# When the scatters of the message stage may begin: TensorE's signals a whole epoch ahead in place of half an epoch

## The chip, the core and the metric
The kernel runs on one core of one Trainium2 chip. The metric is the device time of one launch in microseconds (us). The engines are TensorE (PE), VectorE (DVE), ScalarE (ACT), GpSimd (POOL) and SyncE (SP); each runs its own program in order, and they meet only through semaphores.

## The reference
The kernel computes two message-passing layers of a graph network in float32 on 6250 nodes and 200000 edges, which are sorted by their destination.

The first layer takes the features of each edge's `dst` node and 32 attributes of the edge, and forms a tensor product of 160 values; the messages are added up by the edge's `src` node:

```
tp       = fctp_messages(node_features[col], edge_attr_tensor, W1, W2, W3, W4)
messages = tp @ Wm + bm
agg      = segment_sum(messages, row, N_NODES)
upd      = concatenate([node_features, agg]) @ Wu + bu
x        = layernorm(x + node_features + upd)
```

The second layer gathers by `src`, weights with a small network on 16 edge attributes, averages by `dst`, and ends in a second layer norm. Only the first layer is touched here, and of it the part that makes the messages and writes them to memory in the order of `src`.

## The kernel before
The edges are 1568 tiles of 128. A first part sorts out where the message of each edge goes (`pos_f`, a row number in the table `msgs` in memory, grouped by ranges of `src`). Then comes the message stage (the block from line 1006), and then a stage that reads the table back and sums it (from line 1438), and the second layer.

The message stage works in 98 epochs of 16 tiles (`EP`), each of 8 pairs of tiles (`PAIRS0`). Two buffers alternate by the epoch's parity r. In an epoch n:
- SP loads the attributes (`nat`, 1 MB, line 662) and the node rows (`xw`, line 658).
- DVE masks and turns the attributes (`masks`, lines 1124 to 1133), turns the node products (`products`, line 1139), prepares the selection of nodes two epochs ahead (`select`, line 1147), and in most of the stage works on the positions of later tiles (`places`, lines 1078 to 1115). `masks` of epoch n waits until all messages of epoch n-2 are signalled (line 1121).
- TensorE makes four message pairs (`messages`, line 1346, into the four banks `ps_m`), then the first node products of epoch n+2 (`step_a`, line 1314), then four more pairs, then the other node products (`step_bc`). With the first and second pair it also turns node rows (lines 1308, 1311). Each finished pair raises `s_msg` by one. A pair waits until the pair four before it has left its bank (`s_mev`, line 1339).
- ScalarE waits until the scatters of epoch n-2 have landed (`s_out[r]`, line 1265), puts the positions into `place[r]` (lines 1266, 1269), and copies each finished pair to `stage[r]` (`message`, line 1260, raising `s_mev`). Between the fourth and fifth pair it moves the first node products (`keep_a`, line 1234, three instructions), after the eighth the others (`keep_bc`, seven instructions).
- GpSimd scatters the tiles from `stage[r]` to `msgs`, 128 rows of 648 bytes each, one indirect DMA per tile (line 1045), 16 per epoch. They are two runs of eight: the pairs 0 to 3, and 4 to 7.

GpSimd has two kinds of waits in front of its scatters. One is for data: the pair must have been copied to the stage buffer (`s_mev`, line 1042). The other is about order only: the first scatter of each run also waits for `s_msg`, the count of pairs that TensorE has signalled, at a point further on than the data needs (lines 1038 to 1041). TensorE raises `s_msg` by `PAIRS0` = 8 at the outset (line 1362), so the value n * 8 + 16 stands for all pairs of epochs 0 to n, and n * 8 + 20 for those and the first four of epoch n+1. The last epoch's second run has no such wait.

The scatters of an epoch begin after the wait of ScalarE's position casts and of the data; an epoch's run cannot pass the one before it, since GpSimd issues in order.

Of the kernel before, what the change touches and what calls it, by code (L numbers as in the profile page):

```python
# [570 lines left out]
def gnn_kernel(nc, A, out, scratch):  # L571
# [14 lines left out]
    with outer:  # L586
# [39 lines left out]
        with nc.cleanup_on_exit(), ExitStack() as ctx:  # L626
            sb, ps = sb_in(ctx), ps_in(ctx)

            def sem(n):
                return nc.alloc_semaphore(name=n)  # L630
# [328 lines left out]
            with ExitStack() as main:  # L959
# [18 lines left out]
                s_msg, s_mev, s_loc, s_place = sem("msg"), sem("mev"), sem("loc"), sem("place")  # L978
# [4 lines left out]
                PAIRS0 = EP // 2  # L983
                HALF0 = PAIRS0 // 2
# [21 lines left out]
                with nc.Block() as block:  # L1006
# [18 lines left out]
                    @block.gpsimd  # L1025
                    def _(pool):
                        for r in range(2):
                            nc.gpsimd.memset(by_node[:, r, :, :], 0.0).then_inc(s_blank_y, 1)

                        def scatter(t, r, first=False, last=False):  # L1030
                            n = t * 2 + r
                            if not first:
                                pool.wait_ge(s_out[r], t * (16 * EP))
                                pool.sem_inc(s_begun, 1)
                            pool.wait_ge(s_place, n + 1)
                            pool.wait_ge(s_loc, n + 1)
                            for g in range(PAIRS0):
                                if g == 0:
                                    pool.wait_ge(s_msg, n * PAIRS0 + 2 * PAIRS0)
                                elif g == HALF0 and not last:  # L1040
                                    pool.wait_ge(s_msg, n * PAIRS0 + 2 * PAIRS0 + HALF0)
                                pool.wait_ge(s_mev, n * PAIRS0 + (BANKS + g + 1))
                                pool.sem_inc(s_begun, 1)
                                for k in (2 * g, 2 * g + 1):
                                    nc.gpsimd.indirect_dma_start(out=msgs, out_offset=bass.IndirectOffsetOnAxis(ap=place[:, r, k:k + 1], axis=0),  # L1045
                                                                 in_=stage[:, r, k, :], in_offset=None).then_inc(s_out[r], 16)

                        pool.wait_ge(s_filled, 16 * SRC_BUCKETS)
                        for r in range(2):
                            scatter(0, r, True)  # L1050
                        with pool.Fori(1, EPOCHS // 2 - 1) as t:
                            for r in range(2):
                                scatter(t, r)
                        for r in range(2):
                            scatter(EPOCHS // 2 - 1, r, last=r == 1)
                        for r in range(2):
                            pool.wait_ge(s_out[r], 16 * EP * (EPOCHS // 2))
# [1062 lines left out]
        with ExitStack() as ctx:  # L2120
# [60 lines left out]
            s_msg, s_add = sem("msg"), sem("add")  # L2181
# [421 lines left out]
        with ExitStack() as ctx:  # L2603
# [31 lines left out]
            s_msg = sem("msg")  # L2635
# [616 lines left out]
```

## Time and profile before

| | us |
|---|---|
| median of 3 runs | 5932.78 |
| lowest, highest | 5931.32, 5964.56 |
| the profiled execution, its own time | 5928.51 |
| its span | 5926.9 |

| engine | busy us in the span | share |
|---|---|---|
| PE (TensorE matmul) | 4250.2 | 72% |
| DVE | 3998.3 | 67% |
| POOL (GpSimd) | 3142.6 | 53% |
| ACT | 1158.8 | 20% |

Busy time is the time in which an engine executes something. For GpSimd's scatters it is the time in which the instruction is processed, not that in which the data moves. TensorE's mean granted clock over the span is 0.796 of full speed. A row of the timeline gives the start, the busy time, the engine, the line and the operation with its output and input, the number of instructions that are taken together (xN), and in brackets how long the engine had been idle before, and what released it. "issue" there means that the profile shows no one that it waited for. "remote" stands for another core or an unknown queue.

### The profile page before, as it was taken

The page shows a single profiled execution, that of the slowest core. Times are in us where ns is not written, and L with a number is a line of the kernel's source. Part 1 is how long each engine was busy: PE and PEld are TensorE (multiplying, and loading weights), DVE is VectorE, ACT ScalarE, POOL GpSimd, SP SyncE. Part 2 cuts the span into 40 slices and gives each one's busy share as a digit, 9 for nine tenths or more (in the row PEclk, how much of TensorE's full clock was granted, in tenths as well). Part 3 has the DMA queues.
Part 4 walks back from the last instruction along what each step waited for, and adds up shares of the span by engine and source line. Part 5 has one row for each costly group of instructions (what it writes and reads, how often), then busy time and mean ns, then how long its engine had stood idle before and what let it go on. Part 6 is the DMA issues. An engine that isn't in the chain of part 4 may idle for free. (4 is left out here: it accounts for less than half of the span.)

```text
span 5926.9 us, 109584 instructions
## 1 busy us (share of the span) xinstructions
PE 4250.2 (72%) x32221; PEld 3208.9 (54%) x32221; DVE 3998.3 (67%) x7157; ACT 1158.8 (20%) x3221; POOL 3142.6 (53%) x3256
## 2 busy tenths in 40 slices
PE   4777776777777677769987667666676766777675
PEld 3555555555555455569976445454454544555454
DVE  8888888888888876658864555555555555555554
ACT  1323232322322232300013011111111111111111
POOL 0566666666666666630004555555565555555553
PEclk8778787777777777779988877778777777777877
DMA  5333333333333333359963222222222222222221
GB/s 155 91 100 101 99 100 99 101 99 99 100 100 100 99 100 100 100 184 302 303 192 97 59 58 55 59 55 59 56 58 57 57 56 56 57 59 57 57 58 41
DMA packets 585273, 567.76 MB, mean 96 GB/s; under 512 B 180293, under 2 KB 473638, under 8 KB 584854
## 3 DMA queue, kind: packets, MB, share of 16 engines
q0 software_dynamic: 150528, 258.71, 16.2%
q1 hardware_dynamic: 401238, 230.91, 15.6%
q10 hardware_dynamic: 33408, 76.99, 4.0%
q8 instruction: 42, 0.69, 0.1%
q14 instruction: 57, 0.47, 0.0%
HBM read 407.78 MB, written 158.52 MB: 96 GB/s over the span
## 5 line engine op out<-in xcount | busy, mean ns | idle before, releaser
L2281 POOL DMA_INDIRECT q_fg<-f,q_index x1568 | 1551.6, 990 | 1125.7 <-issue 545.5
L1045 POOL DMA_INDIRECT messages<-stage,place x1568 | 1523.6, 972 | 914.2 <-issue 445.3
L1346 PE MATMUL ps_m<-by_attr,turned 128*128 128x160 f32 x6272 | 1131.1, 334 | 277.1 <-issue 271.9
L1346 PEld LDWEIGHTS ps_m<-by_attr,turned 128*128 128x128 f32 x6272 | 1028.0, 212 | 418.6 <-issue 409.7
L2530 PE MATMUL q_ps_m<-q_prod,q_onehot_sh 128*32 128x160 f32 x12544 | 791.7, 364 | 454.1 <-DVE q_sums L2343 232.8
L2343 DVE SCALAR_TENSOR_TENSOR q_sums<-q_ps_m,split_q,q_sums 128x161 f32 x784 | 301.8, 385 | 1119.3 <-issue 1029.1
L2530 PEld LDWEIGHTS q_ps_m<-q_prod,q_onehot_sh 128*32 128x32 f32 x12544 | 476.5, 129 | 724.7 <-issue 408.7
L2517 PE MATMUL q_ps_w<-q_wfc,q_hidden 64*128 64x192 f32 x3136 | 574.0, 427 | 211.5 <-issue 198.7
L1314 PE MATMUL ps_y<-w_xy,xt 32*128 32x256 f32 (+3 forms) x1176 | 447.0, 650 | 316.8 <-ACT xz L1231 281.8
L1139 DVE STREAM_TRANSPOSE by_attr<-by_node 128x2048 f32<-128x2048 f32 (+1 forms) x294 | 548.1, 1916 | 31.3 <-ACT by_node L1234 17.5
L2517 PEld LDWEIGHTS q_ps_w<-q_wfc,q_hidden 64*128 64x128 f32 x3136 | 364.2, 233 | 337.6 <-issue 298.3
L2427 ACT ACTIVATE q_hidden<-q_ps_h 128x512 f32<-128x512 f32 x196 | 117.0, 597 | 2025.8 <-PE q_ps_f L2539 774.0
L1234 ACT ACTIVATE by_node<-ps_y 128x256 f32<-128x256 f32 (+1 forms) x980 | 376.5, 494 | 499.4 <-remote 272.7
L1544 PE MATMUL ps_g<-rows_in,local 128*128 128x161 f32 x3328 | 458.8, 300 | 13.4 <-DVE local L1495 13.4
L1544 PEld LDWEIGHTS ps_g<-rows_in,local 128*128 128x128 f32 x3328 | 458.5, 190 | 14.6 <-DVE local L1495 14.6
L1130 DVE SCALAR_TENSOR_TENSOR masked<-ps_at,quarter,nat 128x2048 f32<-128x2048 f32 x196 | 460.8, 2351 | 8.3 <-issue 0.3
L1260 ACT COPY stage<-ps_m 128x320 f32<-128x320 f32 x784 | 310.8, 443 | 759.0 <-PE ps_m L1346 359.4
L1133 DVE STREAM_TRANSPOSE turned<-masked 128x2048 f32<-128x2048 f32 x196 | 453.1, 2312 | 6.7
L1314 PEld LDWEIGHTS ps_y<-w_xy,xt 32*128 32x128 f32 (+1 forms) x1176 | 143.9, 217 | 540.9 <-ACT xz L1231 300.6
L2508 PE MATMUL q_ps_h<-q_scal_t,q_wfc 128*128 128x128 f32 x1568 | 327.6, 345 | 147.8 <-issue 120.9
L2330 DVE TENSOR_TENSOR q_prod<-q_ps_w,q_fg 128x384 f32<-128x384 f32 x784 | 396.7, 548 | 0.0
L2508 PEld LDWEIGHTS q_ps_h<-q_scal_t,q_wfc 128*128 128x128 f32 x1568 | 262.3, 239 | 224.4 <-issue 221.0
(270 smaller groups left out, 4098.4 us busy)
## 6 DMA issues: line engine op xcount, KB each, us to landing
nat<-in_edge_attr SPq DMA_DIRECT2D x392, 256.0 KB
rows_in<-messages ACTq DMA_DIRECT2D x208, 324.0 KB, 3.4
rows_in<-messages SPq DMA_DIRECT2D x208, 324.0 KB, 3.4
messages<-stage,place POOLq DMA_INDIRECT x1568
q_fg<-f,q_index POOLq DMA_INDIRECT x1568
q_a<-in_edge_attr SPq DMA_DIRECT2D x196, 64.0 KB
messages<-zeros SPq DMA_DIRECT2D x25, 324.0 KB, 2.9
xw<-in_x SPq DMA_DIRECT2D x98, 80.0 KB
```

The source lines that it names most:

```text
L1045: nc.gpsimd.indirect_dma_start(out=msgs, out_offset=bass.IndirectOffsetOnAxis(ap=place[:, r, k:k + 1], axis=0), in_=stage[:, r, k, :], in_ ...
L1130: nc.vector.scalar_tensor_tensor(masked[:, :, :], at, quarter[:, half:half + 1], nat[:, :, :].rearrange("p t (j w) -> p (t j) w", w=32), A ...
L1133: nc.vector.transpose(turned[:, r, half, :], masked[:, :, :].rearrange("p t w -> p (t w)")).then_inc(s_turn, 1)
L1139: nc.vector.transpose(by_attr[:, r, :, c, :].rearrange("p k c h -> p c k h"), by_node[:, r, c, :]).then_inc(s_attr, 1)
L1314: return nc.tensor.matmul(bank[:, at:at + cols.stop - cols.start], source[rows, :], weights[rows, cols], start=True, stop=True, tile_posit ...
L1346: last = nc.tensor.matmul(ps_m[g % BANKS][:, k % 2 * D0:k % 2 * D0 + D0], turned[:, r, half, k * P:(k + 1) * P], by_attr[:, r, k, :, half] ...
L1544: last = nc.tensor.matmul(ps_g[u % BANKSZ][:, 0:W1_], local[:, u % RINGZ, j, :], rows_in[:, u % RINGZ, j, 0:W1_], start=(j == 0), stop=(j ...
L2281: nc.gpsimd.indirect_dma_start(out=fg[:, i, place_of(v), :], out_offset=None, in_=f_tab, in_offset=bass.IndirectOffsetOnAxis(ap=index[:, i ...
L2330: last = nc.vector.tensor_tensor(prod[:, h % 2, at, part, NS:D0].rearrange("p v (i u) -> p v i u", u=NV), w[:, :, c:c + NV].unsqueeze(2).b ...
L2508: last = nc.tensor.matmul(ps_h[:, a * P:a * P + P], wfc1[:, a, :], scal_t[:, par, :], start=True, stop=True)
L2517: last = nc.tensor.matmul(ps_w[:, g, half, b, 0:192], hidden[rows, par, 2 * g + b, :], wfc2[rows, :], start=True, stop=True, tile_position ...
L2530: nc.tensor.matmul(ps_m[strip, g, 0:D0], oh_sh[:, strip], prod[:, h % 2, g * QUAD + place_of(v), 1 if c < 3 else 0, :], start=(v == 0), st ...
```

## The change
The first scatter of each run waits for a higher count of `s_msg`. For the run of pairs 0 to 3 of epoch n it was n * 8 + 16 (epoch n complete) and is n * 8 + 20 (the first four pairs of epoch n+1 too), except in the last epoch, where it stays. For the run of pairs 4 to 7 it was n * 8 + 20 and is n * 8 + 24 (epoch n+1 complete); the last epoch has no such wait in either kernel. Counted from the end of the run's own pairs, TensorE must have signalled a whole epoch further on, where it was half an epoch.

```diff
                             for g in range(PAIRS0):
                                 if g == 0:
-                                    pool.wait_ge(s_msg, n * PAIRS0 + 2 * PAIRS0)
+                                    pool.wait_ge(s_msg, n * PAIRS0 + 2 * PAIRS0 + (0 if last else HALF0))
                                 elif g == HALF0 and not last:
-                                    pool.wait_ge(s_msg, n * PAIRS0 + 2 * PAIRS0 + HALF0)
+                                    pool.wait_ge(s_msg, n * PAIRS0 + 3 * PAIRS0)
                                 pool.wait_ge(s_mev, n * PAIRS0 + (BANKS + g + 1))
```

## Rows read from the trace of the kernel before

**Rows 1.** Busy time by window, the message stage from the first scatter on:
```profile
core 0: us, PE busy (x) PEld busy (x) DVE busy (x) ACT busy (x) POOL busy (x), PEclk, DMA share, GB/s
172.00:2579.00 2407.00, 1708.37 (x8144) 1250.39 (x8140) 1885.97 (x2099) 703.11 (x2120) 1523.58 (x1568) 0.78 0.38 99
```

**Rows 2.** Groups of instructions, GpSimd in the message stage:
```profile
line engine op names shapes xcount | busy us, mean ns | idle before us <-releasers
L1045 POOL DMA_INDIRECT messages<-stage,place x1568 | 1523.6, 972 | 914.2 <-issue 445.3 <-ACT stage L1260 408.2 <-PE ps_m L1346 57.8
```

**Rows 3.** Timeline, the first scatter and TensorE's matmuls for half 2:
```profile
start us, us, engine line op out<-in xcount [idle before <-releaser]
172.65 1.15 POOL L1045 DMA_INDIRECT messages<-stage,place  x1 [32.23 <-ACT stage L1260]
...
175.41 3.63 PE L1346 MATMUL ps_m<-by_attr,turned 128*128 128x160 f32 x24
```

**Rows 4.** Timeline, GpSimd, first and last scatter behind each kind of boundary:
```profile
185.01 0.96 POOL L1045 DMA_INDIRECT messages<-stage,place  x1 [2.28 <-PE ps_m L1346]
...
195.21 0.97 POOL L1045 DMA_INDIRECT messages<-stage,place  x1 [0.30 <-issue]
...
208.90 0.97 POOL L1045 DMA_INDIRECT messages<-stage,place  x1 [3.81 <-ACT stage L1260]
...
2513.74 0.96 POOL L1045 DMA_INDIRECT messages<-stage,place  x1 [2.38 <-ACT stage L1260]
...
2537.60 0.97 POOL L1045 DMA_INDIRECT messages<-stage,place  x1 [2.47 <-ACT place L1269]
...
2568.26 0.97 POOL L1045 DMA_INDIRECT messages<-stage,place  x1 [0.30 <-issue]
```

**Rows 5.** Timeline, around the boundary at 1071.18:
```profile
1065.31 2.18 PE L1314 MATMUL ps_y<-w_xy,xt 64*128 64x512 f32 x6
...
1067.42 4.77 PE L1346 MATMUL ps_m<-by_attr,turned 128*128 128x160 f32 x32
...
1070.32 0.43 ACT L1260 COPY stage<-ps_m 128x320 f32<-128x320 f32 x1 [5.60 <-PE ps_m L1346]
...
1071.18 0.97 POOL L1045 DMA_INDIRECT messages<-stage,place  x1 [2.38 <-PE ps_m L1346]
...
1076.27 3.63 PE L1346 MATMUL ps_m<-by_attr,turned 128*128 128x160 f32 x24
...
1080.12 0.97 POOL L1045 DMA_INDIRECT messages<-stage,place  x1 [0.30 <-issue]
...
1082.59 0.22 ACT L1266 CAST stage<-loc 128x16 f32 x1 [5.84 <-DMA messages<-stage,place]
```

**Rows 6.** Timeline, behind two runs on end:
```profile
1094.39 4.07 PE L1314 MATMUL ps_y<-w_xy,xt 64*128 64x512 f32 x6 [14.49 <-ACT xz L1231]
...
1095.13 0.97 POOL L1045 DMA_INDIRECT messages<-stage,place  x1 [3.84 <-ACT stage L1260]
...
1098.39 7.41 PE L1346 MATMUL ps_m<-by_attr,turned 128*128 128x160 f32 x32
```

**Rows 7.** Timeline, around the boundary at 283.13:
```profile
281.48 0.28 ACT L1266 CAST stage<-loc 128x16 f32 x1
...
282.46 4.08 PE L1314 MATMUL ps_y<-w_xy,xt 64*128 64x512 f32 x6 [0.23 <-ACT xz L1231]
...
283.13 0.97 POOL L1045 DMA_INDIRECT messages<-stage,place  x1 [5.01 <-ACT stage L1260]
...
286.66 1.57 ACT L1234 ACTIVATE by_node<-ps_y 128x512 f32<-128x512 f32 x3 [3.30 <-PE ps_y L1314]
...
289.00 0.43 ACT L1260 COPY stage<-ps_m 128x320 f32<-128x320 f32 x1 [0.77 <-PE ps_m L1346]
```

**Rows 8.** Timeline, GpSimd, a short pause and the boundary after it:
```profile
847.50 0.97 POOL L1045 DMA_INDIRECT messages<-stage,place  x1 [1.08 <-PE ps_m L1346]
...
860.75 0.97 POOL L1045 DMA_INDIRECT messages<-stage,place  x1 [3.32 <-ACT stage L1260]
```

**Rows 9.** Timeline at 520.60, and busy time by window with the granted clock (0.50, 1.00):
```profile
520.60 4.08 PE L1314 MATMUL ps_y<-w_xy,xt 64*128 64x512 f32 x6 [6.10 <-ACT xz L1231]
...
1094.40:1100.40 6.00, 6.00 (x13) 3.00 (x14) 5.14 (x13) 2.47 (x6) 4.05 (x5) 0.50 0.21 63
1065.30:1071.30 6.00, 6.00 (x34) 4.48 (x34) 5.96 (x5) 0.98 (x3) 3.02 (x4) 1.00 0.83 196
```

## The prediction, made before the changed kernel was run
> **What bounds the kernel now.** I read the busy times by window first, to find the stage that the change touches, then the groups of instructions for the engine whose waits it edits, then the timeline around the boundaries between that engine's runs.
>
> The message stage takes 2407 of the 5926.9 us span [rows 1]. No engine is full in it: DVE is busy 1886 us of it, TensorE 1708, GpSimd 1524. Still GpSimd is the bound. Its 1568 scatters last 972 ns each, and all its idle time is listed with them: 914.2 us [rows 2], 32.2 of it ahead of the first scatter [rows 3]. Inside a run the next scatter starts 0.30 us after the last, so 16 scatters take 16 x 1.27 = 20.4 us. An epoch takes (2537.60 - 172.65) / 96 = 24.6 us [rows 3, 4]. Nearly all of the other 4.2 us are pauses at the boundaries between two runs of eight.
>
> Call the eight scatters of four message pairs run k, and the four pairs half k (k from 0 to 195, even k opens an epoch). The timeline has three kinds among the 195 boundaries [rows 4]:
> - 56 without a pause (0.30 us; first at 195.21, last at 2568.26)
> - 87 after a single run of eight: 214.9 us, mean 2.47 (first at 185.01, last at 2513.74; most are 2.4 to 2.6)
> - 52 after two runs or more on end: 207.7 us, mean 3.99 (first at 208.90, last at 2537.60)
>
> The sum is 16.8 + 214.9 + 207.7 = 439 us, 2.25 per boundary. The 1372 gaps inside runs make up the other 443 of the 882 us that are listed after the first scatter, 0.32 each.
>
> **Why it pauses.** TensorE's signals get through while GpSimd is idle and early in a run, and then they are held until the run has ended. In [rows 5] the message matmuls from 1067.42 on end at 1068.6, 1069.8, 1071.0 and 1072.2, but ScalarE, idle for 5.60 us, gets the message before them only at 1070.32. The run's last scatter ended at 1071.18 - 2.38 = 1068.80, so the release comes 1.5 us behind it. That is also when the scatters' data has landed: the next run has its eighth scatter at 1080.12, it ends at 1081.09, and ScalarE's wait for the landing ends at 1082.59, again 1.5 us. GpSimd needs 0.86 us from the signal to its next scatter (1070.32 to 1071.18). 1.5 + 0.86 = 2.4, the single pause. After two runs on end the release is later: last end 1095.13 - 3.84 = 1091.29, next scatter 3.84 us on [rows 6]. Early in a run signals pass: in the run from 283.13 ScalarE takes node products at 286.66, 0.1 us after the last ends, and a message at 289.00, 5.9 us into the run, with a wait of 0.77 [rows 7].
>
> **The change, part by part.**
> 1. *The threshold.* Run k now waits for half k+2, it waited for half k+1. No instruction is added or removed on any engine or queue; scatters and DMAs stay as they are. The last two runs keep what they had.
> 2. *The boundaries.* For run k+1 to follow without a pause, half k+3 must be signalled before run k or early in it. Take k even. Half k+3 closes an epoch, and TensorE can only go there once ScalarE has moved half k+2 from the banks to the stage buffer, which the scatters up to run k-1 have to leave: this is their landing, 0.9 us before run k starts. ScalarE's casts and copies take 1.0 us to TensorE's start (281.48 to 282.46 [rows 7]), say 1.3 from the release; TensorE takes 2.18 for the node products and 4.77 for four pairs [rows 5]. It is ready 8.3 us after the release, 7.4 into run k. Signals were seen to pass at 5.9 and not at 9.8 (1068.6, in a run from about 1058.9 = 1068.80 - 9.9), so I take it as held. For k odd [rows 5] shows the same work: from the release at 1070.3 to 1076.27 + 3.63 = 1079.9, which is 9.6 us, 8.7 into the run, held too. From one release to the next are 9.9 of run + 2.55 = 12.45 us, so both are ready for it. I expect 193 boundaries at the single pause and the last two at 0.30. I take 2.55 us for it, the usual value; the mean of 2.47 holds a few of 1.1. 193 x 2.55 + 0.6 = 493 us against 439: **+54 us**.
> 3. *The start.* The first scatter at 172.65 waited for epoch 0. Now it waits for half 2, whose last matmul ends at 175.41 + 3.63 = 179.0 [rows 3]; with about 1.1 us to the scatter that is 180.1, **+7.5 us**. GpSimd is the bound from there on, so this stays.
> 4. *Who is queued behind the wait.* On GpSimd itself only scatters. Who waits for those is ScalarE, at the start of each epoch, for the stage buffer, and behind it TensorE for its banks. By step 2 that loop takes 8.3 or 9.6 of 12.45 us and costs nothing while TensorE has its full clock. DVE has 19.2 us of work per epoch (1886 / 98) beside 25.2. ScalarE and SyncE keep their order.
>
> Bounds for the one unknown, the mean boundary: above 3.99 us, if every release is as late as after long runs (+331 us; runs are only eight long now); below 1.08, the pause at 847.50 [rows 8] (-231 us). I take 2.55, by the 87 rows behind a single run.
>
> The release sits on the landing. The Trainium skill ("DMA: Bandwidth & Descriptors", section on the anatomy of one DMA on the SWDGE path) puts the fixed cost of such a DMA at about 2.0 us, most of it the wait for the write receipt. With 2.0 for the measured 1.5 the pause would be 2.9 and the sum some 80 us higher; the trace has 1.5 here twice, and that decides.
>
> Sum: 54 + 7.5 = +61 us on the profiled execution's 5928.5, that is 5990. The median of the three runs lies 4.3 us higher: **5994 us**.
>
> **Rivals.**
> *A. TensorE gets late.* The tight loop leaves TensorE idle for about 6 us before each odd run (ready at 8.3, needed again at 12.45 + 1.9). An idle of 6.10 us was followed by node products of 4.08 us instead of 2.18, and after one of 14.49 us the granted clock was 0.50 (1.2 GHz), where it is 1.00 (2.4 GHz) in steady work [rows 6, 9]. That cold start took 1105.8 - 1094.4 = 11.4 us for work of 7.0, 4.4 more. On 9.6 us this makes 14.0, 1.6 over the 12.45. A second form is a boundary that passes without a pause and is followed by one of 5.01 [rows 7]. If every epoch pays 1.6 us: 61 + 97 x 1.6 = +216, 6149; if half of them do, +139, 6072. Against it: a late TensorE is not idle before its next half, which then runs at full clock, and its signals pass early in the run.
> The Trainium skill has a rule on this side ("TensorE: Matmul & The Clock Gate", part 1): idleness takes the array's clock to half rate. The rows at 520.60 and 1094.39 agree.
> *B. Faster.* Long runs hold the signals longest, and TensorE then idles 14.49 us and restarts cold [rows 6]. Without long runs less is held up, and the release may come before the landing, as at 847.50 with a pause of 1.08 [rows 8]. With half of the boundaries like that: 193 x (2.55 + 1.08) / 2 = 350 us, 89 less than now, with the start -81: 5852. It decides from a mean boundary below 2.2 us. Against it: at the one shown the next boundary cost 3.32, so 2.2 on the average of the two.
> *C. It does little.* Half k+3 often gets through early in run k, long runs stay, and the three kinds average 2.25 to 2.4 as now: 0 to +29 us and the start, about 5955. For it: I have the limit between passed and held only as somewhere between 5.9 and 9.8 us into a run, and my 7.4 lies in it.
>
> **Numbers.** Forecast 0.42, A 0.2, B 0.13, C 0.25. Over or under 1% (59 us: 5874 and 5992) is about what a measurement of this kernel can tell from no change. The forecast's own range is 5965 to 6030 and straddles that line, a little over half of it above. Slower: 0.24 + 0.2 = 0.44. Within: 0.18 + 0.25 and 0.01 of B = 0.44. Faster: 0.12. The range of 5920 to 6085 leaves out B and the upper half of A.
>
> **What would show it.** Right: nearly every boundary of the stage has a pause of 2.4 to 2.6 us, runs of sixteen are gone but for the last, an epoch takes 25.2 us, the first scatter is at 180, the stage ends some 60 us later and everything behind it is as long as before. A: pauses of 3.5 to 5 us at every second boundary, and a granted clock under the 0.78 of [rows 1]. B: pauses near 1 us. C: many boundaries at 0.30. The prediction is wrong in its root if the release of the signals is not tied to the end of a run, which I infer from their times alone.

## The result, and the profile after

| | before | after |
|---|---|---|
| median, us | 5932.05 (5931.11 to 5964.56, 4 runs) | 6193.82 (6177.21 to 6206.17, 4 runs) |
| the profiled execution, us | 5928.51 | 6198.78 |
| its span, us | 5926.9 | 6197.1 |
| mean granted clock of TensorE | 0.796 | 0.782 |

The change makes the kernel slower: ratio 1.0418, 95% interval 1.0396 to 1.044. The forecast was 5994 with a range up to 6085. The sign was forecast; the size was missed by a factor of more than four (+270 us between the profiled executions, +61 forecast).

Busy time by window of the changed kernel, for its message stage, answers to [rows 1]:

```profile
172.00:2828.00 2656.00, 1772.03 (x8132) 1302.19 (x8130) 1882.30 (x2093) 718.04 (x2120) 1528.37 (x1568) 0.75 0.35 90
```

The work is the same (DVE 1882 us, GpSimd 1528), the stage is 249 us longer, and the granted clock in it fell from 0.78 to 0.75. TensorE was busy 1708 us and is busy 1772: the same matmuls, slower.

The group of GpSimd's scatters, which answers to [rows 2]:

```profile
L1045 POOL DMA_INDIRECT messages<-stage,place x1568 | 1528.4, 975 | 1161.8 <-ACT stage L1260 514.4 <-issue 417.5 <-remote 229.8
```

Idle time in front of them rose from 914.2 to 1161.8 us. Timeline of the changed kernel: the first scatter and TensorE's matmuls for half 2 ([rows 3]), then one boundary of each kind in the middle of the stage and the last pause of the stage ([rows 4]):

```profile
172.07 3.63 PE L1346 MATMUL ps_m<-by_attr,turned 128*128 128x160 f32 x24
...
176.86 1.15 POOL L1045 DMA_INDIRECT messages<-stage,place  x1 [39.71 <-ACT stage L1260]
...
986.76 0.97 POOL L1045 DMA_INDIRECT messages<-stage,place  x1 [2.52 <-remote]
...
1001.52 0.97 POOL L1045 DMA_INDIRECT messages<-stage,place  x1 [4.80 <-ACT stage L1260]
...
2796.96 0.97 POOL L1045 DMA_INDIRECT messages<-stage,place  x1 [3.57 <-ACT stage L1260]
```

The three kinds of boundary of before are gone. In their place there are two, and they alternate ("behind a single run" means that the boundary before it had a pause too):

| boundaries | forecast | after |
|---|---|---|
| into an epoch's first run (k even, 97) | 2.55 us each | 93 behind a single run, mean 2.47; sum of all 235.0 |
| into its mid-epoch run (k odd, 98) | 2.55 us each | 94 behind a single run, mean 4.56, most 4.8 to 5.1; sum of all 435.2 |
| without a pause | 2 | 5 |
| sum (before: 439.7) | 493 | 670.1 |
| a steady epoch (before: 24.6) | 25.2 | 27.1 to 27.5, median 27.3 |

Nearly the whole miss is the second row of this table. In every seventh epoch the mid-epoch pause is only 2.4 us, but there GpSimd has stood 2.8 to 3.1 us inside the run before it, behind that run's first scatter, and the epoch is no shorter. (The kernel before stands 1.9 to 2.2 us at these places; why it does is not known.)

The 270.3 us divide as follows. The start is 4.2 later (176.86 against 172.65; it varies from run to run, 180.62 against 169.97 when both were run again as e9 and e10). The boundaries are +230.4. The gaps inside runs are +9.8 (452.0 against 442.2), and the scatters themselves +4.8. These make 249.2, the shift of the stage's last scatter (from 2578.2 to 2827.3). Behind the stage are 21.1 more, 3369.8 against 3348.7. That part runs the same code in every kernel here, and on chips where before takes about 5940 it took 3337 to 3380, so I don't read these 21 us as an effect of the change.

**One epoch in the trace of after.** Here one chain of waits makes a whole epoch. Timeline of the changed kernel, from one mid-epoch run to the next (lines of GpSimd inside the runs left out):

```profile
955.52 1.41 SPq L662 DMA_DIRECT2D nat<-in_edge_attr  x2
...
959.37 0.97 POOL L1045 DMA_INDIRECT messages<-stage,place  x1 [2.51 <-remote]
...
961.73 0.22 ACT L1266 CAST stage<-loc 128x16 f32 x1 [11.33 <-DMA messages<-stage,place]
...
962.72 4.08 PE L1314 MATMUL ps_y<-w_xy,xt 64*128 64x512 f32 x6 [9.17 <-ACT xt L1228]
...
966.73 6.70 PE L1346 MATMUL ps_m<-by_attr,turned 128*128 128x160 f32 x32
...
973.47 0.43 ACT L1260 COPY stage<-ps_m 128x320 f32<-128x320 f32 x1 [0.69 <-PE ps_m L1346]
...
974.32 0.97 POOL L1045 DMA_INDIRECT messages<-stage,place  x1 [5.04 <-ACT stage L1260]
...
981.19 2.42 SPq L662 DMA_DIRECT2D nat<-in_edge_attr  x4
```

Read it as a loop:
- The mid-epoch run of the epoch before ended at 959.37 - 2.51 = 956.86.
- Its data has landed only at 961.73, 4.87 us later. Until then ScalarE stands at its wait of line 1265, idle for 11.33 us, and TensorE behind it for 9.17.
- TensorE starts at 962.72, 0.99 later. Its node products take 4.01 to the first message matmul, and its message matmuls 6.70 (16 of them, which the row counts as 32): it is at half clock.
- The last message is signalled at 973.43, and GpSimd starts the next mid-epoch run 0.89 later, at 974.32.
- That run ends at 986.76 - 2.52 = 984.24 (above), 9.92 later.

4.87 + 0.99 + 4.01 + 6.70 + 0.89 + 9.92 = 27.4 us, the measured distance from 956.86 to 984.24. The mid-epoch run of epoch n now waits for the second half of epoch n+1. TensorE cannot begin that half before ScalarE has put the first half into the stage buffer, and that needs the landing of the mid-epoch run of epoch n-1. So each mid-epoch run waits for the one before it, through four engines, once per epoch. In the kernel before, that same half is needed one run later, by the first run of epoch n+1. From the end of one mid-epoch run the chain then ends with the second next: 4.9 + 1.0 + 10.7 + 0.9 + two runs of 9.9 = 37.3 us for two epochs, 18.7 per epoch. It does not bind at 24.6. (The expectations of e6 and e13 below count this loop as one and a half epochs, 27.4 / 1.5 = 18.3; the count by runs gives two, and either figure lies well under 24.6.)

Two lines of the table of waits, for the long stretch of the stage (us in total, times, longest); the first of after (400 to 2700), the second of before (400 to 2500):

```profile
ACT stage L1266 <- DMA messages<-stage,place: 929.8, 84, 11.5
```
```profile
ACT stage L1266 <- DMA messages<-stage,place: 97.6, 19, 6.0
```

ScalarE waited for a landing 19 times, and now does so in practically every epoch. The stretch from 962.70 to 968.70 of after shows the clock, as [rows 9] does for before:

```profile
962.70:968.70 6.00, 5.98 (x13) 2.97 (x14) 3.40 (x11) 2.50 (x6) 4.48 (x6) 0.50 0.20 66
```

### The profile page after: what moved, and what is told of

It is laid out like the page before. It is cut to its first block and busy times, and to the rows that moved or that the text cites. A ratio compares the mean times of both kernels' runs of the same rounds, so it can differ in the third digit from the quotient of the medians.

```text
span 6197.1 us, 109584 instructions
## 1 busy us (share of the span) xinstructions
PE 4329.7 (70%) x32221; PEld 3260.5 (53%) x32221; DVE 3995.0 (64%) x7157; ACT 1172.5 (19%) x3221; POOL 3150.2 (51%) x3256
## 5 line engine op out<-in xcount | busy, mean ns | idle before, releaser
L1045 POOL DMA_INDIRECT messages<-stage,place x1568 | 1528.4, 975 | 1161.8 <-ACT stage L1260 514.4
L1346 PEld LDWEIGHTS ps_m<-by_attr,turned 128*128 128x128 f32 x6272 | 1088.2, 225 | 182.6 <-issue 173.0
L1346 PE MATMUL ps_m<-by_attr,turned 128*128 128x160 f32 x6272 | 1151.5, 347 | 19.3 <-issue 10.1
L1314 PE MATMUL ps_y<-w_xy,xt 32*128 32x256 f32 (+3 forms) x1176 | 532.7, 777 | 827.4 <-ACT xz L1231 719.5
L1124 DVE CAST ps_at<-rel_t 128x64 f32 (+1 forms) x98 | 22.3, 228 | 625.5 <-PE ps_m L1346 624.7
```

The lines of the kernel that those rows point to most:

```text
L1314: return nc.tensor.matmul(bank[:, at:at + cols.stop - cols.start], source[rows, :], weights[rows, cols], start=True, stop=True, tile_posit ...
L1346: last = nc.tensor.matmul(ps_m[g % BANKS][:, k % 2 * D0:k % 2 * D0 + D0], turned[:, r, half, k * P:(k + 1) * P], by_attr[:, r, k, :, half] ...
```

## The experiments

The runs were made in four sets, e1 to e4, e5 to e8, e9 to e12 and e13 to e16, and each ratio is to the kernel before, run on the same chip in the same set, with its 95% interval in brackets. Before took 5941, 4963, 5947 and 5842 us in them, so only ratios and traces are compared between sets, and the microseconds in the expectations are meant for a chip at 5940. The record names the chips as 10, 3, 15 and 15, so 5947 and 5842 need not be two chips.

**Which of the two thresholds costs.** The first kernel raises only the threshold of an epoch's first run, the second only that of the mid-epoch run.

```diff
# e1_first_only, against before
-                                    pool.wait_ge(s_msg, n * PAIRS0 + 2 * PAIRS0)
+                                    pool.wait_ge(s_msg, n * PAIRS0 + 2 * PAIRS0 + (0 if last else HALF0))
# e2_mid_only, against before
-                                    pool.wait_ge(s_msg, n * PAIRS0 + 2 * PAIRS0 + HALF0)
+                                    pool.wait_ge(s_msg, n * PAIRS0 + 3 * PAIRS0)
```

> Only the epoch's first run waits for half k+2; the mid-epoch run keeps the old threshold. Loop theory (the loss is the mid-epoch run waiting for a half that TensorE cannot begin before the last scatters have landed): the long pauses of 4.95 us at mid-epoch boundaries go, time 5935 to 6010. Rival (each of the two thresholds costs its part): about 6060.

> Only the mid-epoch run waits for half k+2; the epoch's first run keeps the old threshold. Loop theory: the pauses of about 5 us at mid-epoch boundaries stay, time 6130 to 6210. Rival (each threshold its part): about 6060.

Measured: e1 6267.63 us, ratio 1.0556 (1.0521 to 1.0592); e2 6196.11, 1.0430 (1.0393 to 1.0467), before at 5940.94.

e2 alone has the whole loss of the change. Its timeline around one mid-epoch run:

```profile
970.17 0.22 ACT L1266 CAST stage<-loc 128x16 f32 x1 [11.41 <-DMA messages<-stage,place]
...
971.17 4.08 PE L1314 MATMUL ps_y<-w_xy,xt 64*128 64x512 f32 x6 [9.26 <-issue]
...
975.17 6.52 PE L1346 MATMUL ps_m<-by_attr,turned 128*128 128x160 f32 x32
...
982.59 0.97 POOL L1045 DMA_INDIRECT messages<-stage,place  x1 [6.96 <-ACT stage L1260]
```

The same chain, and the same epoch of 27.3 us, though the pauses lie elsewhere: none of its 97 even boundaries has one, and most mid-epoch pauses are 7.0 to 7.3. That is 0.30 + 7.1 where after has 2.5 + 4.9. The loop sets the epoch, and the even pause only takes its part of it. So the even pauses that I forecast correctly in after cost nothing by themselves.

e1 was expected to do little and has the highest ratio of the study. The pauses at the mid-epoch boundaries did go, as expected, but the time did not. Here GpSimd issues all sixteen scatters of an epoch on end, and then waits 7.89 us (the mean of 95 boundaries). Its timeline in the second half of such a run:

```profile
1043.10 0.79 PE L1308 MATMUL ps_m<-sel,xw 128*128 128x128 f32 x2 [4.92 <-DMA xw<-in_x]
...
1050.82 0.43 PE L1346 MATMUL ps_m<-by_attr,turned 128*128 128x160 f32 x1 [2.40 <-issue]
...
1052.92 4.96 PE L1346 MATMUL ps_m<-by_attr,turned 128*128 128x160 f32 x18 [1.68 <-issue]
1052.99 0.43 ACT L1260 COPY stage<-ps_m 128x320 f32<-128x320 f32 x1 [12.32 <-remote]
...
1058.77 0.97 POOL L1045 DMA_INDIRECT messages<-stage,place  x1 [8.46 <-ACT stage L1260]
```

The run ended at 1058.77 - 8.46 = 1050.31. Node rows reach TensorE late, matmuls stand still for 2.40 and 1.68 us without a wait that the trace names, and ScalarE, idle for 12.32 us, gets the next message only 2.7 us after the run's end. What holds TensorE back late in a long run is not settled here (more on it below). What e1 shows is that the loop of the mid-epoch run is not the only way to lose: a threshold that makes all runs sixteen long is worse.

**The landing.** Why does it take 4.9 us here, where [rows 5] has 1.5? SyncE sends the 1 MB load of the attributes as soon as DVE has masked the old ones. In after that falls at 981.19, 3 us before the end of the mid-epoch run (984.24), and so in every steady epoch. For the landing in [rows 5] it had gone out 15 us before the mid-epoch run's end at 1081.09. SyncE's row in the trace of before:

```profile
1065.77 2.37 SPq L662 DMA_DIRECT2D nat<-in_edge_attr  x4
```

The scatters' own DMA packets (48 per scatter in the trace, taken in order of start) show it without ScalarE's wait. In after the last packet of a mid-epoch run ends 3.86 us behind the run (median of 97), and that of an epoch's first run, with no load close ahead of it, 0.99 us behind. The collision is not new: in before it is the other way round, 0.99 behind a mid-epoch run and 3.70 behind a first run, since there the load goes out 3 us ahead of the first run's end (1065.77 against 1068.80 in [rows 5]). A buffer comes free only with the mid-epoch run, so in before nobody waited for the late packets. The change moved the load from the end of one run to the end of the other.

The next kernel is the changed one, with this load held back until DVE has also turned all the node products of the epoch before (`s_attr`, line 1139), which moves it behind the landing.

```diff
# e3_after_late_load, against after
-                                sp.wait_ge(s_mask, t * 4 + 2 * r)
+                                sp.wait_ge(s_attr, t * 6 + 3 * r)
                                 load_attributes(sp, t * 2 + r)
```

> The changed kernel, with the 1 MB attribute load issued after the three product transposes instead of after the masks, some 5.6 us later, so that it is not in the DMA queues when the mid-epoch run's last scatters land. Loop theory with collision: the landing comes about 1.5 us after the run's end instead of 4.9, TensorE starts 3.4 us sooner, the mid-epoch pause goes from 4.95 to 2.5 us, time 5960 to 6010. Rival (the landing is late for its own reasons, or only TensorE's clock matters): no change, about 6190.

Measured: 5960.52 us, ratio 1.0033 (1.0013 to 1.0052). The loss is gone but for 20 us, with both thresholds as in the change. (On a chip like this one what the late load costs by itself was not measured; e7 below did so on another.) Its timeline:

```profile
932.10 0.22 ACT L1266 CAST stage<-loc 128x16 f32 x1 [7.99 <-DMA messages<-stage,place]
...
933.00 0.97 POOL L1045 DMA_INDIRECT messages<-stage,place  x1 [2.47 <-ACT stage L1260]
...
935.33 1.98 SPq L662 DMA_DIRECT2D nat<-in_edge_attr  x4
...
937.30 1.58 ACT L1234 ACTIVATE by_node<-ps_y 128x512 f32<-128x512 f32 x3 [3.30 <-PE ps_y L1314]
...
945.59 0.97 POOL L1045 DMA_INDIRECT messages<-stage,place  x1 [2.67 <-ACT stage L1260]
```

The run ended at 930.53 and landed at 932.10, 1.57 us later (median of the stage 1.50; in after 4.64). The load follows at 935.33. The mid-epoch pause is 2.67 (mean 2.70 behind a single run), and the sum over all boundaries 460 us, against 670. The prediction's 493 was made with just this landing. With its own assumption true its range would have held, but not its picture: 31 boundaries have no pause where it had two, 22 have one under 2 us, and the sum is nearer to the 440 of before than to 493. TensorE restarts at half clock here too (4.08 us for the node products at 933.10, behind 5.83 idle), and the pause is short all the same.

The half dose: of the load's four parts of 256 KB, two stay where they were and two wait.

```diff
# e14_after_halflate (and e8_after_half_late, the same kernel on another chip), against after
                                 sp.wait_ge(s_mask, t * 4 + 2 * r)
-                                load_attributes(sp, t * 2 + r)
+                                load_attributes(sp, t * 2 + r, (0, 1))
+                                sp.wait_ge(s_attr, t * 6 + 3 * r)
+                                load_attributes(sp, t * 2 + r, (2, 3))
```

> The change with two of the four 256 KB attribute loads behind the attribute signal, two still right behind the masks. Loop theory: the landing is late in proportion to the bytes that lie in the queues with the run's last scatters, so about 2.5 to 3.2 us instead of 4.6 (1.5 with no such load), and the mid-epoch pause falls by as much: 6030 to 6100 where before is 5940. Rival (what counts is that a load stands there at all): landing 4.6 and 6190. Rival (the landing has nothing to do with it, the late load helped through SyncE's order): no such middle value, 5960 or 6190.

Measured: 5919.33 us where before took 5841.65, ratio 1.0127 (1.0094 to 1.016); the unchanged after had 1.0457 in the same set (e16 below). It lies between, so the bytes in the queues matter and not SyncE's order alone. It lies lower than expected: the landing is 2.15 us in the median, where I had expected 2.5 to 3.2, and the mid-epoch pause 2.75 (mean behind a single run). Half the bytes leave a fifth of the delay ((2.15 - 1.50) / (4.64 - 1.50); after in the same set, e16, lands at 4.69, which gives the same fifth).

**The landing counted by halves.** The opposite cut: the load stays where it was, but the wait no longer needs the mid-epoch run. The stage buffer's landing is counted for each half, and ScalarE waits for the half that it is about to overwrite. GpSimd's side, left out below, counts each run's scatters apart and waits for the second half's positions before the mid-epoch run.

```diff
# e11_after_split, against after (e12_before_split: the same against before)
-                s_out = [sem(f"out{r}") for r in range(2)]
+                s_out = [[sem(f"out{r}{h}") for h in range(2)] for r in range(2)]
...
-                                if not first:
-                                    act.wait_ge(s_out[r], t * (16 * EP))
-                            nc.scalar.copy(stage[:, r, :, D0 + 1], loc[:, bass.ds(n * EP, EP)]).then_inc(s_loc, 1)
+                            def begin(h):
+                                if not first:
+                                    act.wait_ge(s_out[r][h], t * (8 * EP))
+                                k0 = h * EP // 2
+                                nc.scalar.copy(stage[:, r, k0:k0 + EP // 2, D0 + 1], loc[:, bass.ds(n * EP + k0, EP // 2)]).then_inc(s_loc, 1)
...
+                            begin(0)
...
+                            begin(1)
```

> The changed kernel unchanged, to see its ratio to the kernel before on the chip of this call. Loop theory: on a chip where the kernel before takes about 5940 us, 1.04; on one where it takes about 4963 us, where TensorE's signals are not held back in the runs, the loop run, landing, ScalarE, TensorE, signal still needs 9.9 + 4.7 + 1.0 + 7 to 10.9 + 0.9 = 23.5 to 27.4 us per epoch and GpSimd only 20.4 to 21.5, so the ratio is larger, 1.04 to 1.12. Rival (the cost is the extra pauses at held signals): 1.00 there.

> The kernel before unchanged, for its trace on the chip of this call: on a slow chip pauses of 2.5 and 4 us at the runs' boundaries, on a fast one most boundaries at 0.30 us, and messages that reach ScalarE within 1 us of the matmul in the middle of a run.

> As e5: the changed kernel with the landing counted apart for the two runs of an epoch. Loop theory on a slow chip: mid-epoch pause 2.5 us, 5950 to 6010; on a fast chip as before, within 0.3% of the kernel before. Rival: over 6100 on a slow chip.

> As e6: the kernel before with the same split of the landing. Loop theory on a slow chip: little changes, 5890 to 5960; on a fast chip 0.997 of the kernel before, as seen. Rival: faster by over 1% on a slow chip.

| one chip, before at 5946.94 | us | ratio | mean boundary, us |
|---|---|---|---|
| e9, after again | 6196.02 | 1.0422 (1.0391 to 1.0453) | 3.43 |
| e10, before again (one run) | 5938.77 | | 2.28 |
| e11, after, landing by halves | 5956.52 | 1.0009 (0.9988 to 1.003) | 2.31 |
| e12, before, landing by halves | 5945.61 | 0.9988 (0.9968 to 1.0008) | 2.32 |

With the loop cut, the changed thresholds cost nothing that can be measured (e11 against e12: 0.2%), and the pattern of before is back: 59 boundaries without a pause, 81 behind a single run with a mean of 2.5 us, 55 behind longer ones with a mean of 4.1. Without the new thresholds the cut brings nothing. Timeline of e11:

```profile
924.74 0.97 POOL L1048 DMA_INDIRECT messages<-stage,place  x1 [2.50 <-ACT stage L1264]
...
927.09 0.21 ACT L1272 CAST stage<-loc 128x8 f32 x1 [1.30 <-DMA messages<-stage,place]
...
948.91 0.97 POOL L1048 DMA_INDIRECT messages<-stage,place  x1 [4.03 <-ACT stage L1264]
```

The wait for the late landing at 927.09 (4.85 us after the run's end at 922.24) is still there in this epoch, but it is now that of the second half, and ScalarE loses 1.30 us in it instead of 11.

**The clock.** Does the cold TensorE share in the loss? Extra matmuls of no use, into a bank whose content is overwritten, fill TensorE's wait in each epoch, 26 in one kernel and 14 in the other. A row of the timeline counts each matmul on float32 as two, here as in the rows of before.

```diff
# e4_after_fill, against after (e15_after_fill14: range(14))
+                                pe.wait_ge(s_ev, (n + 2) * YEV)
+                                for _ in range(26):
+                                    nc.tensor.matmul(ps_y[0][:, 0:D0], turned[:, r, 0, 0:P], by_attr[:, r, 0, :, 0], start=True, stop=True)
```

> The changed kernel, with 26 extra matmuls per epoch (128x160, into a bank of ps_y that is overwritten next) in TensorE's idle time of about 9 us before step_a; their results are not used. Loop theory with clock: step_a and four pairs take 7.0 us instead of 10.8, the mid-epoch pause goes from 4.95 to 2.5 us, time 5960 to 6010. Rival (the late landing alone sets the pause): the pause stays over 4.5 us, about 6190 or above.

> The change with 14 extra 128x160 matmuls of no use in TensorE's wait ahead of each logits chunk (their product is overwritten). They take some 1.9 us at the low clock. Loop theory with the cold matmuls as one term: the logits and message matmuls still begin cold or nearly so with 14, so less than the 2.3 us of 26 fillers is given back: mid-epoch pauses 4 to 4.8 and 6130 to 6200. Rival (clock is no part of the loss): 6195 and pauses as in the changed kernel. Rival (14 suffice for the full clock): pauses of 2.7 as with 26, no long pauses behind unpaused boundaries, and 6000 to 6080.

Measured: e4 6213.51 us, ratio 1.0473 (1.0404 to 1.0543); e15 6146.37 with before at 5841.65, ratio 1.0508 (1.0476 to 1.054). Neither total improves. The trace of e4 shows why this is no answer for 26 fillers. An undisturbed epoch of e4:

```profile
1025.74 3.81 PE L1357 MATMUL ps_y<-by_attr,turned 128*128 128x160 f32 x26
...
1028.71 0.22 ACT L1266 CAST stage<-loc 128x16 f32 x1 [11.32 <-issue]
...
1029.71 2.18 PE L1314 MATMUL ps_y<-w_xy,xt 64*128 64x512 f32 x6 [0.16 <-ACT xz L1231]
...
1031.82 4.75 PE L1346 MATMUL ps_m<-by_attr,turned 128*128 128x160 f32 x32
...
1039.09 0.97 POOL L1045 DMA_INDIRECT messages<-stage,place  x1 [2.82 <-ACT stage L1260]
```

The landing is as late as ever (1028.71 - 1023.80 = 4.91), but TensorE is warm: 2.18 and 4.75 us at a granted clock of 1.00 (1029.7 to 1036.6), where after has 4.08 and 6.70. The mid-epoch pause falls to 2.82 and the epoch to 25.2 us from 27.4. In 20 epochs, though, an even boundary passes without a pause, and the one after it takes longer in most, in 17 of them 11 to 19 us. Here is one:

```profile
1178.75 0.30 PE L1357 MATMUL ps_y<-by_attr,turned 128*128 128x160 f32 x1 [1.12 <-issue]
...
1182.13 0.22 ACT L1266 CAST stage<-loc 128x16 f32 x1 [13.10 <-issue]
...
1186.55 0.42 PE L1357 MATMUL ps_y<-by_attr,turned 128*128 128x160 f32 x1 [3.10 <-issue]
...
1191.17 4.08 PE L1314 MATMUL ps_y<-w_xy,xt 64*128 64x512 f32 x6
...
1202.20 0.97 POOL L1045 DMA_INDIRECT messages<-stage,place  x1 [14.73 <-ACT stage L1260]
```

TensorE crawls through the last fillers, ten instructions from 1177.33 to 1191.17, with starts 0.7 to 3.5 us apart and nothing to wait for. The real work could start a microsecond after 1182.13 and starts at 1191.17. So the fillers made a loss of their own, 263 us in the 20 pauses, which ate their gain.

With 14 fillers the node products still take 4.08 and the messages 6.75 us, the mid-epoch pause is 4.68, and nothing is gained. The pause is in the range that the loop theory gave (4 to 4.8 us). Its figure of 6130 to 6200 was for a chip at 5940, and as a ratio (up to 1.044) it is exceeded by 1.0508. In that set after itself had 1.0457, and the two intervals overlap, so this run cannot tell the loop theory from its rival that the clock is no part of the loss.

What follows: in undisturbed epochs a warm TensorE shortens the epoch by 2.2 us, and an early landing (e3) by as much: either one alone brings the mid-epoch pause down to 2.5 to 2.8 us. The loss needs both, a late landing and a cold TensorE. For the landing a total shows it (e3, e11); for the clock it is read from the undisturbed epochs of e4 alone, and no total does.

**The threshold the other way.**

```diff
# e13_own_half, against before
-                                    pool.wait_ge(s_msg, n * PAIRS0 + 2 * PAIRS0)
+                                    pool.wait_ge(s_msg, n * PAIRS0 + PAIRS0 + HALF0)
                                 elif g == HALF0 and not last:
-                                    pool.wait_ge(s_msg, n * PAIRS0 + 2 * PAIRS0 + HALF0)
+                                    pool.wait_ge(s_msg, n * PAIRS0 + 2 * PAIRS0)
```

> The kernel before with both thresholds half an epoch lower, one step the other way: first run of epoch n at n*34 + 51, mid-epoch run at n*34 + 68. Loop theory: the chain landing, stage, TensorE's half, signal is spread over two epochs instead of one and a half and still does not bind, so no gain beyond what the boundaries of the kernel before cost for other reasons: 5850 to 5950 where before is 5940, and mean boundary pause near 2.2 or a little lower. Rival (early signals matter, every half epoch of threshold costs the same 250 us): 5690. Rival (runs that begin early hold TensorE more than they save): over 6000.

> The changed kernel again, as the yardstick of this call: 1.04 of the kernel before where that takes 5940, with a mean boundary pause of 3.4 us. Where the chip is one on which before takes 4963, the loop theory expects the same sign: with a landing of 2.2 to 2.8 us and matmuls nearer the full clock the chain is 22 to 24 us against epochs of 20, so 1.03 to 1.08. Rival (the loss is only of the chips at 5940): 1.00 there.

The thresholds of e13 are n * 8 + 12 and n * 8 + 16, as the diff has them, and not the n*34 + 51 and n*34 + 68 of the expectation. Measured: e13 5856.51 us, ratio 1.0024 (1.0005 to 1.0042); e16 6120.06, 1.0457 (1.0422 to 1.0491), before at 5841.65. Half an epoch less of lead changes nothing of note (mean boundary 2.14), half an epoch more costs 4.6%. Of the three settings only the highest costs more than 0.4%, and it is the one at which the loop closes: a step and no slope.

**A faster chip.** In one set before took 4963 us. The pauses of the message stage are shorter there.

> The changed kernel, with the landing counted apart for the two runs of an epoch: ScalarE fills the stage buffer's first half once the run of pairs 0 to 3 two epochs back has landed, and only the second half waits for the run of pairs 4 to 7 (four short position casts per epoch in place of two). Loop theory: TensorE's second half no longer hangs on the last landing, the mid-epoch pause goes from 4.95 to 2.5 us although the attribute load stays where it is; time 5950 to 6010. Rival (the attribute load costs by itself, not through the landing): over 6100.

> The kernel before, with the same split of the landing and the old thresholds. Loop theory: with the old thresholds the loop through the landing closes over one and a half epochs, 27.4 / 1.5 = 18.3 us per epoch, and does not bind, so little changes: 5890 to 5960. Rival (the landing is felt in the kernel before too, through TensorE's cold restarts): faster by over 1%, under 5870.

> The kernel before with the attribute load 5.6 us later, old thresholds. Loop theory: not binding there, within 1% of before, 5880 to 5960. Rival (the late load is worth 3.4 us per epoch wherever it stands): about 5700.

> The changed kernel with two of the four quarters of the attribute load issued at the old place and two after the product transposes. Loop theory with a collision in proportion to the bytes ahead: landing about 3.1 us after the run's end, mid-epoch pause 3.3 us, time 6010 to 6090. Rival (any load ahead delays the landing as much as the whole): about 6190; other rival (only the last quarters count): about 5965.

| before at 4963.04 | us | ratio | mean boundary, us |
|---|---|---|---|
| e5, after, landing by halves | 4960.94 | 0.9996 (0.9987 to 1.0006) | 0.70 |
| e6, before, landing by halves | 4950.83 | 0.9973 (0.9962 to 0.9983) | 0.79 |
| e7, before, late attribute load | 5144.27 | 1.0357 (1.034 to 1.0375) | 1.41 |
| e8, after, half of the load late | 5219.81 | 1.0506 (1.0489 to 1.0524) | 1.97 |

e5 confirms e11: with the loop cut, the thresholds cost next to nothing on this chip either (0.2% against e6). e7 and e8 missed their expectations, which were within 1% of before and at most 1.025 of it. e8 is the kernel of e14. Its epochs take (2532.6 - 176.3) / 98 = 24.0 us here and (2616.9 - 180.4) / 98 = 24.9 there, much the same. But e6, which takes about as long as before, has 21.4 on this chip, and before has 24.6 in [rows 3, 4]. The landing is the same too (2.19 and 2.15 us). So one and the same loop costs 5% here and 1.3% there, because the kernel around it is faster here. e7 shows what holding the load back does where the loop is open: alone on before it costs 3.6%, so late loading is no remedy, only a probe. Nor is it a probe that takes the collision away everywhere. In before it moves the load from the first run's end to some 3 to 5 us ahead of the mid-epoch run's end:

```profile
1030.50 1.98 SPq L662 DMA_DIRECT2D nat<-in_edge_attr  x4
...
1032.62 0.97 POOL L1045 DMA_INDIRECT messages<-stage,place  x1 [0.30 <-issue]
...
1038.33 0.22 ACT L1266 CAST stage<-loc 128x16 f32 x1 [4.33 <-DMA messages<-stage,place]
```

The mid-epoch run ends at 1033.59 and lands 4.74 us later (median 4.75). From 400 to 2300 us TensorE also waits 556 us for node rows, and DVE 211 us for the attributes. Which of these makes the 3.6% was not taken apart. After itself was never run on this chip. e6 is the only kernel that beat the one before, by 0.3% on this chip, and on another (e12) the interval includes no change. I did not find a version worth recommending over the kernel before.

## Why the prediction was wrong

1. **The threshold** (step 1): right. No work was added; GpSimd's scatters and all matmuls have their counts.
2. **The boundaries** (step 2): this is the step that failed. It asked the right question, when TensorE has half k+3 ready for k even, and took the right chain, landing, ScalarE, TensorE. Its answer was 7.4 us into run k. The trace has 973.43 - 959.37 = 14.1, behind the end of a run of 9.9. Two terms were mis-sized:
   - The landing of run k-1 was put 0.9 us before run k starts, and comes 2.36 after (961.73 - 959.37): +3.3 us. I had the 1.5 us from one row of [rows 5] and its neighbour, and took it for a constant. It holds where no attribute load goes out close ahead of the run's end. In [rows 5] this load went out earlier, at 1065.77, 15 us before the end of the mid-epoch run; in every steady epoch of after it goes out 3 us before.
   - The node products and messages were costed at 2.18 + 4.77, the warm values, and take 4.01 + 6.70: +3.8 us. TensorE had been idle for 9.17.
   - ScalarE's part came out 0.3 shorter (0.99 for 1.3). 7.4 + 3.3 + 3.8 - 0.3 = 14.2.

   The single pause of 2.55 held where nothing else was late: 2.47 at the even boundaries. "The release sits on the landing" did not hold. At 959.37 GpSimd went on 2.51 us after its run's end, with the landing still 2.4 us away. The release of TensorE's signals follows the end of the run by about 1.6 us (2.47 - 0.86). The rows of before could have told them apart: the release at 1070.32 stands behind the run that ended at 1068.80, and the packets of that run end only at 1072.68.
3. **The start** (step 3): +7.5 forecast, +4.2 measured (+10.7 between e10 and e9). TensorE reached half 2 earlier than before, with its message matmuls at 172.07 instead of 175.41.
4. **"That loop takes 8.3 or 9.6 of 12.45 us and costs nothing while TensorE has its full clock"** (step 4): wrong by its own condition. I checked the loop against one run, with warm durations and the short landing. Counted from the release, as there, it needs 4.87 + 0.99 + 10.71 - 1.6 = 15.0 us against the 12.45 of a run and a pause. The 2.5 us too much are what the mid-epoch pause has above the single one (5.0 against 2.5).

**The rivals.** *A* named the mechanism of half the miss, a TensorE that restarts cold and gets late at every second boundary, and its trace signs came true (pauses of 3.5 to 5 us at every second boundary, a granted clock below 0.78). But its price was 1.6 us per epoch and its total 6149, since it had the short landing too. It had the idle at 6 us, where it is 9, and its objection, that a late TensorE would find its next half warm, did not help the loop. I gave it 0.2, and its upper half lay outside my range. *B* and *C* did not happen. Runs of sixteen did all but vanish, as the forecast had it: five boundaries have no pause, two were forecast. That the kernel got slower at all, as forecast, says little for the sum: its +54 us for the boundaries came from a pattern that did not occur at the mid-epoch boundaries. One what-if of the prediction is off by itself: a pause of 2.9 in place of 2.55 adds 68 us over 193 boundaries, not 80. Nothing hangs on it.

The Trainium skill ("TensorE: Matmul & The Clock Gate", part 1) says that an idle array falls to half rate. I had cited it under A and not applied it to my own step 2, where the idle time in front of the node products followed from the same arithmetic. The rows agree with it (4.08 us behind 9.17 of idle, 2.18 behind the fillers).

**What stays open.** What slows TensorE late in a long run of scatters (e1, e4) was not found, nor what holds its signals back until a run has ended. The share of the clock in the loss is read from epochs of e4 only. After was not run on the faster chip. Why half of the load's bytes leave only a fifth of the delay is not known.

## What to carry to other kernels

Before raising a threshold that only sets order, follow the data all the way round: who must free a buffer so that the awaited work can be done, and is it the waiting engine's own last output? If so, add up every term of that loop per period, with the durations that hold in the new order (cold engine, loaded queues), and compare it with the period. A latency read from one quiet row is a lower bound; look at where the large transfers stand now and where they will stand once the order is changed. Here one of them slid from the end of a run that nobody waited for to the end of the one that frees the buffer.

## What the runs showed of the hardware

- A landing depends on what else is in the queues: a run's last scatters landed 1.50 us after the last one (median, e3) with no load beside them, 2.15 with 512 KB (e14), and 4.64 with 1 MB sent some 3 us before (after). The Trainium skill ("DMA: Bandwidth & Descriptors", section on the anatomy of one DMA on the SWDGE path) has about 2.0 us as the fixed cost of one transfer. The 1.50 us count from the end of GpSimd's last scatter instruction; from its start they are 2.47, so the page's figure lies between the two. The 3.1 us on top in after are traffic: without the load (e3) they are gone.
- While GpSimd runs its scatters, signals of TensorE that come late in a run reach the other engines about 1.6 us after the run's end (pauses of 2.4 to 2.6 us at 92 of the 97 even boundaries of after), and this is not the landing, which comes 4.87 us after the end in the epoch shown. It is not so on every chip: on the fast one, with the changed thresholds, 137 of 195 boundaries have no pause (e5).
- TensorE, with nothing to wait for, started ten matmul instructions in 13.8 us in the second half of a long run of scatters and behind it (e4, 1177.33 to 1191.17), where otherwise 26 of them take 3.81 us (at 1025.74).
- The same kernel, before, took 4963 us on one chip, 5941 on another, and 5947 and 5842 in two sets on what the record names as a third. The scatters last 0.97 us in all of them; on the fast chip the mean boundary pause is 0.70 and 0.79 us (e5, e6), and for the same two kernels on another 2.31 and 2.32 (e11, e12). That is not most of the difference: between the profiled executions of e12 and e6 it is 1003 us, of which 319 are in the message stage and 687 behind it (3366 against 2679). One chip at 4963 was seen once, so nothing here says what makes it fast.
